# A language-model block on one core: the shared expert reads transposed, normalized tokens from DRAM that attention stored there

## What is computed

```
h = table[x]                                   # table: sine rows or weight rows
h = h + attention(layernorm(h))                # 8 heads of 64, heads mixed before and after the softmax
x2 = layernorm(h)                              # [16384, 128]
shared = gelu(x2 @ Ws1 + bs1) @ Ws2 + bs2      # 128 -> 512 -> 128
y = shared + bank(x2, "sp") + bank(x2, "fq")   # two banks of 8 experts, top-1, capacity 1280
out = h + y
```

## Time and profile before

| what | us |
|---|---|
| median of 3 runs | 1618.86 (1616.02 to 1620.89) |
| the profiled execution | 1619.74 |
| its span, first to last instruction | 1618.0 |
| setup, until the first tile is scored | 0 to 102 |
| attention and the head of the shared expert | 102 to 1113 |
| the experts | 1118.8 to 1403.6 |
| the shared expert's stage | 1411.5 to 1618.0 |

### The profile page before, as it was taken

The page is one execution under the profiler, slowest core; times in us unless marked ns, Lnnn a source line. Parts: engine busy times, 40 slices in busy tenths (PEclk is TensorE's granted clock), DMA queues, the critical chain, the costliest instruction groups (busy, mean ns, idle before and its releaser), DMA issues. The chain is left out here.

```text
span 1618.0 us, 37768 instructions
## 1 busy us (share of the span) xinstructions
PE 1506.4 (93%) x11213; PEld 1385.0 (86%) x11213; DVE 1102.4 (68%) x2864; ACT 1155.7 (71%) x3447; POOL 1023.8 (63%) x1068
## 2 busy tenths in 40 slices
PE   5559999999999999989999999987999999699999
PEld 2149999999889989989989999977999999699998
DVE  6767787878777868867877887752333333288888
ACT  5549888888878878878878888854555555355554
POOL 5866558788778768768868777562756655522221
PEclk9689999999999999999999999998999999899999
DMA  6322212211211111100000000001333324244444
GB/s 228 137 101 112 94 53 68 68 54 57 59 42 57 58 40 55 42 25 14 15 14 14 15 14 9 4 5 47 84 95 101 82 74 126 58 132 124 118 123 117
DMA packets 157799, 110.63 MB, mean 68 GB/s; under 512 B 28115, under 2 KB 145341, under 8 KB 157616
## 3 DMA queue, kind: packets, MB, share of 16 engines
q1 hardware_dynamic: 140208, 88.25, 18.1%
q0 software_dynamic: 17408, 20.16, 4.6%
HBM read 54.23 MB, written 70.17 MB: 77 GB/s over the span
## 5 line engine op out<-in xcount | busy, mean ns | idle before, releaser
L914 ACT ACTIVATE expd<-masked,nmax 128x128 f32<-128x128 f32 x1024 | 395.9, 393 | 0.0
L725 POOL TENSOR_TENSOR prob<-expd,rtotal 128x1024 f32<-128x1024 f32 x128 | 242.9, 1898 | 156.4 <-DVE rtotal L992 156.0
L1009 DVE COPY_PREDICATED masked<-off_diag,ps_s 128x1024 f32<-128x1024 int32 x128 | 175.0, 1368 | 149.8 <-PE ps_s L812 149.8
L854 PE MATMUL ps_o<-u,probT 128*128 128x128 f32 x2048 | 249.2, 275 | 0.7 <-issue 0.7
L854 PEld LDWEIGHTS ps_o<-u,probT 128*128 128x128 f32 x2048 | 239.1, 192 | 0.9 <-issue 0.9
L914 ACT ACTIVATION_READ_ACCUMULATOR expd<-masked,nmax 128x1 f32 x1024 | 196.9, 192 | 0.0
L937 ACT ACTIVATE probT<-ps_ut 128x1024 f32<-128x1024 f32 x128 | 131.5, 1027 | 69.6 <-PE ps_ut L820 63.1
L923 ACT ACTIVATE u<-ps_ut 128x1024 f32<-128x1024 f32 x128 | 131.4, 1027 | 69.2 <-PE ps_ut L865 69.2
L1024 DVE TENSOR_TENSOR w_lo<-ps_w,w_hi 128x512 fp32r<-128x512 f32 x256 | 164.2, 681 | 5.9 <-ACT w_hi L944 5.8
L944 ACT ACTIVATE w_hi<-ps_w 128x512 fp32r<-128x512 f32 x256 | 146.7, 596 | 17.6 <-PE ps_w L842 10.6
L1015 DVE TENSOR_REDUCE nmax<-masked 128x8 f32<-128x1024 f32 x128 | 155.6, 1216 | 2.5
(11 more groups left out here) (228 smaller groups left out, 4094.9 us busy)
## 6 DMA issues: line engine op xcount, KB each, us to landing
answers_sp<-zeros SPq DMA_DIRECT2D x16, 512.0 KB
answers_fq<-zeros SPq DMA_DIRECT2D x16, 512.0 KB
sh_back<-answers_sp SPq DMA_DIRECT2D x56, 128.0 KB, 2.2
sh_back<-answers_fq SPq DMA_DIRECT2D x56, 128.0 KB, 2.3
out<-res SPq DMA_DIRECT2D x56, 128.0 KB, 1.9
h_sb<-in_L_tok_weight SPq DMA_DIRECT2D x12, 512.0 KB, 5.1
table<-h_sb SPq DMA_DIRECT2D x12, 512.0 KB
sent_sp<-zeros SPq DMA_DIRECT2D x8, 660.0 KB, 3.0
```

Source lines behind the costliest of these rows:

```text
L725: nc.gpsimd.tensor_tensor(prob[k % 2][:, :].rearrange("p (g j) -> p g j", g=H), expd[k % 2][:, :].rearrange("p (g j) -> p g j", g=H), rtot ...
L854: mm = nc.tensor.matmul(ps_o[:, 0:D], probT[k % 2][:, g * N:(g + 1) * N], u[k % 2][:, g * D:(g + 1) * D], start=(g == 0), stop=(g == H - 1))
L914: ins = nc.scalar.activation(expd[(k - 1) % 2][:, g * N:(g + 1) * N], masked[(k - 1) % 2][:, g * N:(g + 1) * N], ACT.Exp, bias=nmax[(k - 1 ...
L1009: nc.vector.copy_predicated(masked[k % 2][:, :].rearrange("p (g j) -> p g j", g=H), off_diag[:, :].unsqueeze(1).to_broadcast([P, H, N]), p ...
```

## The change

Attention gives `x2T` a second buffer, and SyncE stores each quad's `x2T` to a new DRAM tensor `turned`. In the shared expert's stage SyncE loads one group's half of such a quad, four steps ahead. The `x` tiles, their normalization on VectorE, the transposes on TensorE and the PSUM banks `ps_x` are gone from that stage. `xT_hi` and `xT_lo` are made from the loaded SBUF tile. GpSimd's addition of b2 no longer waits. SyncE's clearing of `answers` in attention is spread: one transfer behind each store of a quad. The wait for all scatters now stands after the first three loads of `xT`, and the tiles of the head come one step later.

```diff
+    turned = nc.dram_tensor("turned", (TILES // 4, P, 4 * P), F32).ap()
 # attention
-        x2T = sb("x2T", [P, 4 * N])
+        x2T = [sb(f"x2T{k}", [P, 4 * N]) for k in range(2)]
+        s_kept = [sem(f"a_kept{k}") for k in range(2)]
 # attention, SyncE
-            for b in range(BANKS):
-                a_t = answers[b].rearrange("(p n r) d -> n p r d", p=P, r=CLEAR_ROWS)
-                for n in range(CLEARS):
-                    sp.wait_ge(S["scored"], BANKS * FILLS + 2 * (b * CLEARS + n + 1))
-                    sp.dma_start(a_t[n], zeros[:, 0:CLEAR_ROWS, 0:D]).then_inc(s_cleared, 16)
+            def clear(n):
+                a_t = answers[n // CLEARS].rearrange("(p n r) d -> n p r d", p=P, r=CLEAR_ROWS)
+                sp.dma_start(a_t[n % CLEARS], zeros[:, 0:CLEAR_ROWS, 0:D]).then_inc(s_cleared, 16)
+
+            for q in range(QUADS):
+                sp.wait_ge(S["x2T"], q + 1)
+                sp.dma_start(turned[q], x2T[q % 2][:, :]).then_inc(s_kept[q % 2], 16)
+                clear(q)
+            for k in range(2):
+                sp.wait_ge(s_kept[k], 16 * QUADS // 2)
 # attention, ScalarE
-                    need(act, S["logit"], q)
-                    nc.scalar.activation(x2T[:, :], ps_x[:, :], ACT.Copy).then_inc(S["x2T"], 1)
+                    need(act, S["logit"], q - 1)
+                    need(act, s_kept[(k - 11) // 4 % 2], (i * (BODY // 8) + (k - 11) // 8) * 16)
+                    nc.scalar.activation(x2T[(k - 11) // 4 % 2][:, :], ps_x[:, :], ACT.Copy).then_inc(S["x2T"], 1)
 # shared_ffn
-        x = [sb(f"x{k}", [P, 2, D]) for k in range(2)]
+        xT = [sb(f"xT{k}", [P, G]) for k in range(BACK)]
-        ps_x = [s.enter_context(nc.psum_tensor(f"sh_ps_x{k}", [P, 512], F32)) for k in range(2)]
 # shared_ffn, SyncE
+            def load_x(i, a):
+                need(sp, S["xlo"], group(i, a) - BACK + 1)
+                q = (i * BODY + HEAD + a) // 2 if isinstance(i, int) else i * (BODY // 2) + (HEAD + a) // 2
+                at = slice(a % 2 * G, (a % 2 + 1) * G)
+                sp.dma_start(xT[a % BACK][:, :], turned[bass.ds(q, 1), :, at].rearrange("o p n -> (o p) n")).then_inc(s_x[a % BACK], 16)
+
             def step(i, k):
+                a = k + 4
+                if live(i, a):
+                    load_x(i, a)
+                if isinstance(i, int) and group(i, k) == -2:
+                    for r in range(RING):
+                        sp.wait_ge(s_scattered[r], 32 * ALL // RING)
 # shared_ffn, TensorE
-                if live(i, k + 1):
-                    c = (k + 1) % 2
-                    need(pe, S["rows"], group(i, k + 1) + 1)
-                    need(pe, S["xlo"], group(i, k))
-                    for b in range(2):
-                        mm = nc.tensor.transpose(ps_x[c][:, b * P:(b + 1) * P], x[c][:, b, :], ident[:, :])
-                    mm.then_inc(S["turned"], 1)
 # shared_ffn, ScalarE
-                    need(act, S["turned"], group(i, k) + 2)
+                    act.wait_ge(s_x[(k + 1) % BACK], (i * (BODY // BACK) + (k + 1) // BACK + 1) * 16)
-                    nc.scalar.activation(xT_hi[c][:, :], ps_x[c][:, 0:G], ACT.Copy).then_inc(S["xhi"], 1)
+                    nc.scalar.activation(xT_hi[c][:, :], xT[(k + 1) % BACK][:, :], ACT.Copy).then_inc(S["xhi"], 1)
 # shared_ffn, VectorE
-                if live(i, k + 2):
-                    need(dve, S["turned"], group(i, k) + 1)
-                    for b in range(2):
-                        t = tile(i, k + 2, b)
-                        ins = nc.vector.tensor_scalar(x[k % 2][:, b, :], h_sb[:, bass.ds(t * D, D)],
-                                                      norm2[:, bass.ds(t * 2, 1)], norm2[:, bass.ds(t * 2 + 1, 1)],
-                                                      ALU.subtract, ALU.mult)
-                    ins.then_inc(S["rows"], 1)
-                    nc.vector.tensor_tensor(xT_lo[c][:, :], ps_x[c][:, 0:G], xT_hi[c][:, :].bitcast(F32), ALU.subtract).then_inc(S["xlo"], 1)
+                    nc.vector.tensor_tensor(xT_lo[c][:, :], xT[(k + 1) % BACK][:, :], xT_hi[c][:, :].bitcast(F32), ALU.subtract).then_inc(S["xlo"], 1)
 # shared_ffn, GpSimd
                 if live(i, k):
-                    need_apart(pool, S["rows"], group(i, k) + 1)
                     at = bass.ds(tile(i, k, 0) * D, 2 * D)
```

More of the change, by code:

```diff
@@ L169, in build @@
             attention(nc, banks[0], banks[2], first, C, table, sent, ident, h_sb, ids, slots,
-                      gates, norm2, x2, to_row, mats, masked, off_diag, zeros, s_zeroed, answers, s_cleared)
+                      gates, norm2, x2, to_row, mats, masked, off_diag, zeros, s_zeroed, answers, s_cleared, turned)
         res = [keep(f"res{k}", [P, 2, D]) for k in range(RING)]
@@ L173, in build @@
         experts(nc, banks, first, sent, x2, to_row, answers, ident, res, tokens, s_scattered, s_cleared)
-        shared_ffn(nc, first, answers, ident, h_sb, gates, norm2, res, s_scattered, out.rearrange("b n d -> (b n) d"))
+        shared_ffn(nc, first, answers, turned, h_sb, gates, res, s_scattered, out.rearrange("b n d -> (b n) d"))
 class RouterConstants:
@@ L603, in attention @@
 def attention(nc, bank, shared, first, C, table, sent, ident, h_sb, ids, slots, gates, norm2,
-              x2, to_row, mats, masked, off_diag, zeros, s_zeroed, answers, s_cleared):
+              x2, to_row, mats, masked, off_diag, zeros, s_zeroed, answers, s_cleared, turned):
     BODY, FIRST, LAST, LEAD, END = 16, 2, 7, 12, TILES + 20
@@ L788, in step @@
                         c = LOGIT_COL + ((k - 12) % BATCH + b) * RE
-                        mm = nc.tensor.matmul(ps_o[:, c:c + RE], x2T[:, b * N:(b + 1) * N], C.wr[:, :], start=True, stop=True)
+                        mm = nc.tensor.matmul(ps_o[:, c:c + RE], x2T[(k - 12) // 4 % 2][:, b * N:(b + 1) * N], C.wr[:, :], start=True, stop=True)
                     mm.then_inc(S["logit"], 1)
@@ L1377, in _, with shared_ffn @@
             looped(pool, step)
-def shared_ffn(nc, first, answers, ident, h_sb, gates, norm2, res, s_scattered, out):
+def shared_ffn(nc, first, answers, turned, h_sb, gates, res, s_scattered, out):
     G = GROUP
@@ L1401, in shared_ffn @@
         one_part, one_out = sb("one_part", [P, D]), sb("one_out", [P, D])
-        ps_x = [s.enter_context(nc.psum_tensor(f"sh_ps_x{k}", [P, 512], F32)) for k in range(2)]
         ps_h = [s.enter_context(nc.psum_tensor(f"sh_ps_h{k}", [P, FC, G], F32)) for k in range(2)]
         ps_o = [s.enter_context(nc.psum_tensor(f"sh_ps_o{k}", [P, 512], F32)) for k in range(2)]
-        S = {n: sem(n) for n in ("rows", "turned", "xhi", "xlo", "up", "gelu", "down", "based", "half", "part", "out",
+        S = {n: sem(n) for n in ("xhi", "xlo", "up", "gelu", "down", "based", "half", "part", "out",
                                  "one_back", "one_based", "one_part", "one_out", "one_put")}
@@ L1408, in shared_ffn @@
         s_back = [sem(f"back{k}") for k in range(BACK)]
+        s_x = [sem(f"x{k}") for k in range(BACK)]
         block = s.enter_context(nc.Block())
@@ L1423, in head_tile @@
         def head_tile(i, k):
-            if isinstance(i, int) and k in (-3, -1, 1):
-                return (2 * HEAD - 2, 2 * HEAD - 1, 0)[(k + 3) // 2], (k + 3) // 2
-            if k % 4 != 1 or not live(i, k):
+            if isinstance(i, int) and k in (-2, 0, 2):
+                return (2 * HEAD - 2, 2 * HEAD - 1, 0)[(k + 2) // 2], (k + 2) // 2
+            if k % 4 != 2 or not live(i, k):
                 return None
@@ L1432, in _ @@
         def _(sp):
-            for k in range(RING):
-                sp.wait_ge(s_scattered[k], 32 * ALL // RING)
-            def step(i, k):
+            def load_x(i, a):
[3 more added lines that the diff above has]
+                sp.dma_start(xT[a % BACK][:, :], turned[bass.ds(q, 1), :, at].rearrange("o p n -> (o p) n")).then_inc(s_x[a % BACK], 16)
+            def step(i, k):
+                a = k + 4
[4 more added lines that the diff above has]
+                        sp.wait_ge(s_scattered[r], 32 * ALL // RING)
                 if head_tile(i, k):
```

## The result

| | before | after |
|---|---|---|
| median (us) | 1618.81 (1615.76 to 1620.89, 7 runs) | 1612.82 (1611.07 to 1614.98, 7 runs) |
| the profiled execution | 1619.74 | 1614.98 |
| its span | 1618.0 | 1613.2 |
| the shared expert's stage begins | 1411.45 | 1416.28 |
| length of that stage | 206.5 | 196.9 |

The ratio is 0.9967 with an interval of 0.9955 to 0.9979. The kernel is faster by 6.0 us, where 7.7 were forecast. The last two rows tell more than the total: the stage that the change is made for is 9.6 us shorter, and it begins 4.8 us later. The experts between attention and this stage take the same time: their first transpose (1126.0, before 1121.1) and their last (1395.7, before 1390.8) both lie 4.9 us later than before.

The account below looks back on a forecast made before the run. VectorE was taken to bound the shared expert's loop at 3.60 us a group, TensorE close behind at 3.42. Later start, burst groups at 4.2 and the rest at 3.18 gave a 7.7 us gain, so 1611, range 1599 to 1622 (8 in 10).

Parts of the forecast that it names:

- TensorE's group of 3.18: Shared expert's stage: without its two transposes TensorE needs 3.18 us a group instead of 3.42, the new floor.
- One burst of additions: Start of the shared expert's stage: GpSimd does all 56 additions, no longer held back, in one row of 52.7 us.
- VectorE's group of 4.2 in the burst: Shared expert's stage: beside the additions VectorE's two-SBUF-input instructions wait, so a group costs 2.55 + 1.66 = 4.2 us.
- First `part` 1.3 us later: Beginning of the shared expert's stage: first `part` at 1420.5, 1.3 us later than now, bounds 0.5 and 3.
- Loads at nothing: Shared expert's stage: one more load per group, issued four steps ahead, costs nothing.
- From first to last `part`: Shared expert's stage: 55 groups, 10.4 in the burst and 44.6 at 3.18 us; 194.4 us before.
- Attention at 0: Attention: the added stores and moved clearings cost 0 us, bounds -1 and +4.
- The harmless burst: Rival, shared expert's stage: VectorE gets in between additions, every group takes 3.18 us; time 1600.7, chance 0.22.
- The whole hold: Rival, shared expert's stage: each VectorE instruction pays an addition's full cost, 4.65 to 5.1 us a group; 1616.4, chance 0.22.
- both engines hold each other up: Rival, shared expert's stage: VectorE also delays GpSimd, burst grows to 64 us; 1625, chance 0.12 together with the clock's fall.
- The rival of the clock: Shared expert's stage: TensorE's clock falls in the burst, 6.4 us a group; 1622.7, chance 0.12 together with mutual hold-up.
- The undisturbed prices of the prediction: Shared expert's stage: VectorE's group without normalization costs 3.07 us with one addition, 2.55 without, both under TensorE's 3.18.

Follow-up runs that it names:

- paced: The changed kernel, with each GpSimd addition waiting for VectorE's `part` of the group before it; 1603.15 us, ratio 0.9908.
- att_all: The changed kernel's attention with the shared expert's stage of the kernel before; 1623.02 us beside 1618.77 for before, ratio 1.0031.
- att_late: As `att_all`, but each store and clearing in attention is issued three tiles later, away from the loop edge; 1617.13 us, ratio 0.9989.

## Why the forecast held, and where it was wrong

The time came at 1612.8 where 1611 was forecast, and by the mechanism that was forecast. That it came within 2 us is luck in part. Two errors of opposite sign stand behind the small difference: the stage gave 9.6 us and not 7.7, and attention cost 4.8 and not 0.

- **TensorE's group of 3.18:** 3.16. The measured group is 0.26 shorter than the 3.42 of the earlier trace rows, so 0.22 for two transposes was a little low, as the step said.
- **One burst of additions:** right. Length 52.7, measured 49.9. The 5.2 us for twelve edges of GpSimd's loop were wrong: four additions in a row take 3.13 us, and no such gap is seen. On the other side the 56 additions lay (49.9 - 16 x 0.45) / 56 = 0.76 apart, and not 0.72.
- **VectorE's group of 4.2 in the burst:** 4.36. Groups in the burst: 10.4, measured about ten in 41.5 us, which is 4.15 each.
- **First `part` 1.3 us later:** counted from the start of the stage it comes 9.68 us in, where before it came 7.79 us in, so 1.9 later, within the bounds. The three first loads take 2.26 us to issue. In `paced` the first one landed after 3.49 us, where the step took 2.2 from a load in the middle of the stage.
- **Loads at nothing:** right. The group of 3.16 holds with four loads.
- **From first to last `part`:** 194.4 before, 185.4 forecast, 182.6 measured. Of this the ten groups of the burst took 41.5 and the others 141.1.
- **Attention at 0:** this is the step that failed. The bounds of -1 to +4 just miss the +4.2 of `att_all`. The step rested on the earlier trace rows, and said that traffic costs nothing since two long stretches have the same pace at 60 and 14 GB/s. What the rows show is right, and it holds between the edges still. But the first stretch, to 440, ends where the first edge begins. The second holds two edges, and the 7.54 us in which TensorE is idle there are just the waits of these two (1.48 and 2.62, 0.82 and 2.62). I took the pace of the whole stretch and didn't look at what these waits depend on, nor at what the change issues ahead of them. The source tells it: the copy to `x2T` stands at the step next to the edge, and the clearing is now issued behind the store, 512 KB right after 256 KB.
- **The rivals.** The harmless burst falls: 4.36 us a group and not 3.18. The whole hold falls: it needed 4.65 to 5.1. That both engines hold each other up is in the rows, but it is small: the additions lie 0.76 apart and not 1.0. The Trainium skill ("SBUF — State Buffer", "Who interferes with whom") says that "Issue order, not op shape, decides who blocks." The pairs of up to 1.57 us beside 0.60 alone fit VectorE blocking. GpSimd's additions don't: the longest took 0.97 us and the median 0.778, against 0.73 undisturbed. Here the measurement decides. The rival of the clock came in small: it held at 1.00 for 34.84 us at 82% busy, and then fell to 0.50 for some 3 us at the end of the burst, for at most 1.9 us of time. I gave it little, and priced it for the whole burst.

The undisturbed prices of the prediction, 3.07 for VectorE with one addition a group, also say what `paced` showed: one addition a group would have been free all along. I had the number, and did not draw this from it.

What stays open: whether the engines at an edge wait for just the packets of the instruction queues; whether the store and the clearing cost by their 768 KB or by standing right behind each other; why `att_late`, with nothing ahead of its third edge, still waits 1.46 us there; and what sets how long the clock stays low behind an edge.

## What to carry to other kernels

When a wait is removed because its data dependency is gone, ask what pace it gave: here a wait for a buffer kept GpSimd's work spread, one addition to a group, and without it the same work became a burst that cost 9 us. When transfers are moved, look at where in the loop they are issued and not only at how many bytes move: stores of 256 KB and clearings of 512 KB, issued together just ahead of a loop's four edges, cost 5.9 us more than three tiles later, while either alone cost nothing that could be told. A busy table over a long stretch proves nothing for the short places in it.

## What the runs showed of the hardware

- At the edges of attention's loop the engines wait for nothing that semaphores explain, TensorE for 0.8 to 2.2 us and then once more for 2.1 to 2.6. The first of these waits was 0.79 to 1.52 us with 512 KB or less issued ahead of the edge, and 1.81 to 2.23 with 768 KB in two transfers, issued some 8 us ahead of the end of the wait. At the first edge the three packets of the queue q8 took 0.90 us each with nothing beside them (`att_late`) and 1.28 with the 768 KB.
- A GpSimd addition of 128x256 float32 costs a VectorE instruction with two SBUF inputs about 0.5 us (`xT_lo` 0.42 and then up to 0.95, a pair of L1540 0.60 and then 1.17), and in an unbroken row of additions a pair takes up to 1.57. GpSimd pays much less: 0.05 us an addition at the median (0.778 beside 0.730).
- TensorE kept its full clock (1.00, 2.4 GHz) over 34.84 us in which it was busy for 82%. Then, behind a wait of 2.26 us, it was granted 0.50 (1.2 GHz) for at least 3.2 us.
